# Attention on Trainium2: two PSUM banks for the scores and three for the raw products, with the prior added to the scores first

## The reference

```
x = L0_attn_x                                             # 32 x 256 x 128, float32
x = x + 0.5 * ffn(layernorm(x), ...)                      # routed experts, top 2 of 12 (4 of them zero experts)
x = x + attn(layernorm(x), Wq, bq, Wk, bk, Wv, bv, Wo, bo, prior_lambda)
x = x + 0.5 * ffn(layernorm(x), ...)

# attn, 16 heads of 8, L = 256
Q, K, V = split_heads(x @ Wq.T + bq), ...
scores = einsum('bhqd,bhkd->bhqk', Q, K) / sqrt(8)
scores = scores + prior_lambda * gaussian_mask(256)       # the same for all heads and batches
out = einsum('bhqk,bhkd->bhqd', softmax(scores), V)
return out @ Wo.T + bo
```

## Time and profile before

| | |
|---|---|
| median of 3 runs | 1354.19 us (1350.55 to 1358.74) |
| span of the profiled execution | 1338.4 us |
| PE, DVE, ACT, POOL busy | 75%, 68%, 54%, 46% of the span |
| exponentials (L849) | 512, 595 ns each |
| maxima (L1329) | 512, 685 ns each |
| turns, first score to last exponential | 160.9 to about 1209 us, with six expert blocks in between |

### The profile page before, as it was taken

The page is one execution under the profiler, slowest core; times in us unless marked ns, Lnnn a source line. Parts: engine busy times, 40 slices in busy tenths (PEclk is TensorE's granted clock), DMA queues, the critical chain, the costliest instruction groups (busy, mean ns, idle before and its releaser), DMA issues.

```text
span 1338.4 us, 37494 instructions
## 1 busy us (share of the span) xinstructions
PE 1003.1 (75%) x13558; PEld 656.9 (49%) x13558; DVE 906.0 (68%) x2405; ACT 716.5 (54%) x1486; POOL 621.8 (46%) x697
## 2 busy tenths in 40 slices
PE   1468587788778888888888888898888876774770
PEld 1346243475447544574444754454754465433560
DVE  4548776685566787866887758877867853654524
ACT  1157344567355755667556575555675555442650
POOL 2556256404544544354542544544445445543554
PEclk9989699998788999998999889988999987785886
DMA  8354535352135311362112731123621274130464
GB/s 247 78 125 107 152 98 173 70 131 55 58 68 131 84 52 60 82 149 60 48 58 65 141 87 53 47 61 73 137 81 53 62 162 113 48 90 19 110 145 113
DMA packets 248881, 125.30 MB, mean 94 GB/s; under 512 B 124384, under 2 KB 238925, under 8 KB 248448
## 3 DMA queue, kind: packets, MB, share of 16 engines
q1 hardware_dynamic: 232320, 94.01, 27.2%
q0 software_dynamic: 16384, 28.89, 8.9%
HBM read 36.25 MB, written 65.31 MB: 76 GB/s over the span
## 4 chain that ended last, share of the span: by engine, by line
PE 39%; DVE 27%; issue 15%; ACT 8%; another core or an unknown queue 7%; POOL 2%; DMA 1%; SPq 1%; DVEq 0%; POOLq 0%; ACTq 0%
PE banks L594 10%; DVE row_max L1329 9%; PE banks L623 4%; PE banks L569 3%; ACT probs L849 3%; DVE h_lo L1223 3%; PE banks L561 2%; PE banks L474 2%; ACT h_hi L778 2%; PE banks L431 2%; PE banks L472 2%; PE banks L487 2%; PE banks L490 2%; DVE stats L1094 2%
## 5 line engine op out<-in xcount | busy, mean ns | idle before, releaser
L849 ACT ACTIVATE probs<-banks 128x512 f32<-128x512 f32 x512 | 280.1, 595 | 313.0 <-PE banks L594 270.4
L1329 DVE TENSOR_REDUCE row_max<-banks 128x2 f32<-128x512 f32 x512 | 330.9, 685 | 100.5 <-PE banks L594 65.2
L938 POOL DMA_INDIRECT big<-yg,slots x256 | 255.2, 997 | 278.3 <-ACT y_rows L784 84.0
L924 POOL DMA_INDIRECT xg<-xs,slots x256 | 253.6, 991 | 274.7 <-PE banks L594 167.8
L1223 DVE TENSOR_TENSOR h_lo<-h_f,h_hi 128x512 bf16<-128x512 f32 x198 | 134.5, 688 | 156.7 <-ACT h_hi L778 118.5
L623 PE MATMUL banks<-probs,v_op 128*32 128x256 f32 x2048 | 202.2, 413 | 10.7 <-ACT ot_sb L842 3.0
L569 PE MATMUL banks<-q_op,k_op 32*128 32x256 bf16 x1024 | 152.2, 293 | 64.7 <-issue 46.0
L594 PE MATMUL banks<-band_parts,thirds 96*32 96x296 bf16 (+2 forms) x4096 | 189.7, 294 | 1.3 <-issue 1.3
L487 PE MATMUL banks<-w_all,h_hi 128*128 x792 | 157.6, 229 | 43.1 <-DVE h_lo L1223 21.6
L561 PE MATMUL banks<-k_op,q_in 32*128 32x256 bf16 x1024 | 154.7, 295 | 37.8 <-DVE row_max L1329 31.5
L776 ACT ACTIVATE h_f<-banks 128x512 f32<-128x512 f32 x198 | 119.8, 605 | 114.3 <-PE banks L474 71.5
(11 more groups left out here) (173 smaller groups left out, 1668.6 us busy)
## 6 DMA issues: line engine op xcount, KB each, us to landing
yg<-y_rows SPq DMA_DIRECT2D x198, 128.0 KB
k_op<-kq_kept SPq DMA_DIRECT2D x96, 64.0 KB
q_in<-kq_kept SPq DMA_DIRECT2D x96, 64.0 KB
xg<-zeros SPq DMA_DIRECT2D x2, 2944.0 KB
xg<-xs,slots POOLq DMA_INDIRECT x256
big<-yg,slots POOLq DMA_INDIRECT x256
kq_kept<-kq_hi SPq DMA_DIRECT2D x32, 128.0 KB
kq_kept<-kq_lo SPq DMA_DIRECT2D x32, 128.0 KB
```

The lines of the kernel that those rows point to most:

```text
L849: act.activation(probs[:, q % 2, u % 4, :], banks[:, ST[(16 * b + u) % 3], :], ACT.Exp).then_inc(A["exp_done"], 1)
L924: pool.indirect_dma_start(xg[q], bass.IndirectOffsetOnAxis(slots[:, q % 4, c, t:t + 1], 0), xs[:, q % 2, t, :], None, bounds_check=groups[ ...
L938: pool.indirect_dma_start(y_back[:, i, c, :], None, yg[q], bass.IndirectOffsetOnAxis(slots[:, q % 4, c, t:t + 1], 0)).then_inc(gathered[i] ...
L1329: dve.tensor_reduce(row_max[:, gp, :, qt, j], banks[:, MX[v % 2], :].rearrange("p (k c) -> p k c", k=2), AX.X, ALU.max).then_inc(A["max_do ...
```

## The change

The ring of banks for scores goes from three to two, (0, 1), and the ring for raws from two to three, (2, 3, 4). The waits that guard the banks move with them: a score now waits for the exponential of the unit two before it (three before it till now), and a raw waits for the maximum of the unit three before it (two before it till now). In each step the 16 bands change places: the eight of the scores come first, the eight of the raws second. Nothing is added or taken away.

```diff
-        ST, MX, PV, M = (0, 1, 4), (2, 3), 5, (6, 7)
+        ST, MX, PV, M = (0, 1), (2, 3, 4), 5, (6, 7)
...
-                return pe.matmul(banks[:, MX[v % 2], bass.ts(k, L)],
+                return pe.matmul(banks[:, MX[(16 * rb + v) % 3], bass.ts(k, L)],
...
-                return pe.matmul(banks[:, ST[(16 * b + u) % 3], bass.ts(k, L)], k_op[r:r + 32, par, g, bass.ts(kt, P)],
+                return pe.matmul(banks[:, ST[u % 2], bass.ts(k, L)], k_op[r:r + 32, par, g, bass.ts(kt, P)],
...
-                                wait(pe, A["exp_done"], 16 * b + u + i - 2)
+                                wait(pe, A["exp_done"], 16 * b + u + i - 1)
                             score_half(b, par, u + i, k)
                         if rb is not None:
                             if k == 0:
-                                wait(pe, A["max_done"], 16 * rb + v + i - 1)
-                            raw_half(rpar, v + i, k)
+                                wait(pe, A["max_done"], 16 * rb + v + i - 2)
+                            raw_half(rb, rpar, v + i, k)
...
-                    if raws:
-                        prior_to_raws(v)
                     if main:
                         prior_to_scores(b, 2 * s)
+                    if raws:
+                        prior_to_raws(rb, v)
...
-                            act.activation(probs[:, q % 2, u % 4, :], banks[:, ST[(16 * b + u) % 3], :],
+                            act.activation(probs[:, q % 2, u % 4, :], banks[:, ST[u % 2], :],
```

More of the change, by code:

```diff
@@ L555, in project, with raw_half @@
                 mm.then_inc(A["kq_done"], 1)
-            def raw_half(par, v, k):
+            def raw_half(rb, par, v, k):
                 gp, qt, j = v // 8, v % 8 // 4, v % 4
                 r, g = 32 * j, 2 * gp + k
-                return pe.matmul(banks[:, MX[v % 2], bass.ts(k, L)],
+                return pe.matmul(banks[:, MX[(16 * rb + v) % 3], bass.ts(k, L)],
                                  q_in[r:r + 32, par, g, bass.ts(qt, P)], k_op[r:r + 32, par, g, :],
@@ L601, in prior_to_scores, with prior_to_raws @@
                     for r in range(4):
-                        mm = add_band(ST[(16 * b + u) % 3], u % 8 // 4, r)
+                        mm = add_band(ST[u % 2], u % 8 // 4, r)
                     mm.then_inc(A["st_done"], 1)
-            def prior_to_raws(v0):
+            def prior_to_raws(rb, v0):
                 for v in (v0, v0 + 1):
                     for r in range(4):
-                        mm = add_band(MX[v % 2], v % 8 // 4, r)
+                        mm = add_band(MX[(16 * rb + v) % 3], v % 8 // 4, r)
                     mm.then_inc(A["raw_done"], 1)
@@ L1315, in _ @@
             attention_constants()
-            MX, M = (2, 3), (6, 7)
             def batch_stats(b):
@@ L1328, in maxima @@
                     wait(dve, A["cols_ready"], 2 * b + gp - 1)
-                dve.tensor_reduce(row_max[:, gp, :, qt, j], banks[:, MX[v % 2], :].rearrange("p (k c) -> p k c", k=2),
+                dve.tensor_reduce(row_max[:, gp, :, qt, j], banks[:, MX[(16 * b + v) % 3], :].rearrange("p (k c) -> p k c", k=2),
                                   AX.X, ALU.max).then_inc(A["max_done"], 1)
```

## The result

The changed kernel takes 1346.47 us in the median (1341.83 to 1358.86, 12 runs) against 1354.61 us for the kernel before on the same chip (12 runs): 8.1 us less. The forecast was 1343 us.

The account below looks back on a forecast made before the run. The prediction took a loop of PE waiting for raws' banks and DVE for their bands to bound steps 0 to 2 of light turns; 8.8 us (light) plus 2 us (heavy) off 1354.19 gave 1343.4 us, range 1338 to 1348.

Parts of the forecast that it names:

- The opened loop: Steps 0 to 2 of light turns: PE's raws wait for DVE's maxima, a 2.03 us period that a third raw bank opens.
- the closed one: Steps 0 to 2: with two score banks, the second score waits for the step before's second exponential, a 1.83 us period.
- The 0.23 us for the maxima's later start: Each step: with the raws' bands second, DVE starts its maxima about 0.23 us later than by the old order.
- A free light turn: Light turn without holds: three periods shrink 0.60 us, 0.1 taken off for step 4; gain 0.5 us, bounds 0 and 0.99.
- the chain starts from the bands: After step 3: the path to kq_lo starts from bands, not maxima, so kq_lo comes 0.6 us earlier if a_xt_lo is ready.
- The held turns: Light turns where POOL's DMA delays PE's increments: period 2.09 us, gain 0 to 0.8; 0.4 us mean over 22 light turns, 8.8.
- rival 1: Light turns: held increments and later maxima eat the gain; 0.1 us x 22, nothing in heavy turns, about 1352 us; chance 0.28.
- the heavy ones: Ten turns with two POOL DMAs per step: 0.2 us x 10 = 2 us gain, bounds 0 and 16 us.
- the sum of 8.8 and 2: Whole kernel: 8.8 us from 22 light turns plus 2 us from 10 heavy turns, 10.8 us less.
- What the waits were to show: New profile: PE's raw-bank waits (31.5, 57.4 us) near nothing, PE's score waiting for ACT instead, ACT's 270.4 us band wait falling.
- rival 2: Steps 0 to 3: DVE starves as maxima come later; 15 us price at most, 10 expected, 1364 us; chance 0.16.
- Rival 3: Heavy turns gain as well, ACT and DVE being decoupled by half a step: 14 us there, 1331 us; chance 0.13.

Follow-up runs that it names:

- both halves of the change: The new banks with the old order of bands, and the old banks with the new order, each against the kernel before: ratios 1.0052 and 1.0184.
- without the DMAs: Kernel before and changed kernel, each skipping the 288 indirect DMAs POOL issues during the turns: 1267.3 and 1256.03 us, against 1357.94 us for before with them.
- banks alone: Kernel before with two score banks and three raw banks, the raws' bands still first: 1216.58 us against 1210.75 us for before, ratio 1.0052.
- order alone: Kernel before with its three score banks and two raw banks, but the scores' bands first: 1232.98 us against 1210.75 us for before, ratio 1.0184.
- interleaved: Changed kernel with bands unit by unit (score, raw, score, raw): 1199.13 us against 1210.75 us for before, ratio 0.9908; again on another chip 1347.88 us, 0.9926.
- the first set: Follow-up runs on one chip: the change again 1202.18 us, new banks only 1216.58, new order only 1232.98, unit-by-unit bands 1199.13, before 1210.75.

## Why the prediction was right, and where it was off

**The loops.** The step that carried the forecast was right in kind and size. The opened loop (2.03 us) and the closed one (1.83 us by the sum, 1.81 to 1.82 measured) are confirmed by both halves of the change, whose periods the same terms give (2.06 and 2.26). The 0.23 us for the maxima's later start was 0.22 to 0.25 us. One reading was too smooth: turn 10 was not free, since between 514.69 and 517.11 in the earlier trace rows lie 2.42 us and not 2.03; without the DMAs all three periods are 2.02 to 2.03.

**A free light turn.** Forecast 0.5 us, measured 0.57 (18.50 to 17.93 us), and by the path that was forecast. The bands of steps 0 and 3 of turn 11 (L594 is L602 in these two kernels), without the DMAs, before and then the change, cut the stretch between two kq_lo (above) in three:

```profile
488.64 0.56 PE L602 MATMUL banks<-band_parts,thirds 96*32 96x180 bf16 x13
...
494.71 0.64 PE L602 MATMUL banks<-band_parts,thirds 96*32 96x180 bf16 x16
```

```profile
477.51 0.56 PE L602 MATMUL banks<-band_parts,thirds 96*32 96x180 bf16 x13
...
482.96 0.64 PE L602 MATMUL banks<-band_parts,thirds 96*32 96x296 bf16 x16
```

| us | kq_lo to bands of step 0 | three periods | bands of step 3 to kq_lo |
|---|---|---|---|
| before | 9.46 | 6.07 | 2.97 |
| change | 9.51 | 5.45 | 2.97 |
| banks alone | 9.28 | 6.18 | 2.97 |
| order alone | 9.65 | 6.80 | 2.97 |
| interleaved | 9.28 | 5.45 | 2.97 |

The three periods give 0.62 us (forecast 0.60) and the part behind kq_lo takes 0.05 back (forecast 0.1). The last part is the same in all five kernels, and so are the 1.24 us in it from the bands to the projections: as forecast, the chain starts from the bands, and a_xt_lo does not lead in these turns. In turn 11 of the change it ends at 549.78, and the projections start at 550.15, 0.37 us later, where 0.82 - 0.43 = 0.39 had been reckoned. DVE's wait ahead of kq_lo fell by 0.43 us because the maxima of step 3 moved towards kq_lo; it is not a measure of the gain. Between step 3 and the next step 0 the bands shift, which I had no terms for (3 to 4 takes 0.43 us more, 4 to 5 takes 0.61 less, 5 to 7 takes 0.39 less, 7 to 0 takes 0.61 more), but this nearly cancels. The table also shows what interleaving adds: its 0.23 us are all ahead of step 0.

**The held turns.** This step was right in its numbers and wrong in what it gave. I had forecast a period of 2.09 us with maxima that come with the release; turn 14 shows 2.05 and 2.09 us and maxima at 0.98 us. But the turn gains nothing: from the first bands to kq_lo it took 9.49 us before and takes 9.48 now. Its three periods are 0.5 us shorter in all, and the last part is 0.5 us longer (3.53 us instead of 3.03). The DMA of step 3, released sooner, now covers the end of the projections (670.95, when they end at 671.79), so kq_hi starts 0.57 us after that end; before, the DMA came at their end and kq_hi followed 0.10 us behind. The later a_xt_lo has hardly a part in it: the projections start 1.28 us after the bands, 1.24 before. Such a turn ends as rival 1 says, but by another path. Not all do: on the same stretch turns 13 and 15 gain 0.34 and 0.12 us. What is left over the whole shows in the sums of the light turns that have no expert block between them (17 of the 18; from one start of kq_lo to the next, the last one, from turn 27 to 28, left out):

| 17 light turns, 7 heavy ones, us | before | change | interleaved |
|---|---|---|---|
| chips of 1354 to 1358 us | 351.3, 355.1; 168.4, 169.6 | 349.1; 172.5 | 347.2; 168.3 |
| the same without the paced DMAs | 335.9; 132.1 | 329.1; 127.1 | |
| chip of 1211 us | | 332.0; 129.9 | 327.4; 128.3 |

(Two executions of before in the first row. Banks alone: 339.6; 133.2. Order alone: 346.2; 140.9. The first two of the seven heavy stretches end with the second kq_lo, ahead of turn 0, and with that of turn 0.) With the DMAs these 17 light turns gain 2 to 6 us, where 17 x 0.4 = 6.8 was forecast, and the heavy ones take 3 to 4 us more in the profiled executions, where a gain of 2 was forecast; without the DMAs 6.8 and 5.0 us are gained. So the DMAs, not the nature of the heavy turns, keep those from gaining. The holds alone may not be the whole of it: on the chip of 1211 us, where hardly any increments come late, the change gains 8.6 us and so hardly more than on the first. The medians say 8.1 us in all, which is more than the rows place: expert blocks differ by over 10 us between two executions of before on two chips (five of them with their turns, 381.9 and 393.4 us), and one profile each can't divide 8 us among stretches. That the sum of 8.8 and 2 came within 3 us of the measured gain is therefore in part luck: the term of a free turn is confirmed, the 0.4 us as a mean over held turns and the 2 us of the heavy ones are not.

**The clock.** I had left it out. A turn with a stretch at half the clock loses 0.7 to 1.3 us. In the changed kernel without the DMAs (columns as in the earlier trace rows):

```profile
595.50:615.00 19.50, 16.29 (x303) 9.41 (x296) 17.65 (x43) 11.23 (x23) 2.09 (x4) 0.98 0.12 36
615.00:635.40 20.40, 17.31 (x304) 10.05 (x300) 17.51 (x43) 11.32 (x23) 2.09 (x4) 0.92 0.12 35
613.00:617.60 4.60, 3.46 (x56) 2.02 (x57) 3.28 (x8) 1.19 (x3) 0.00 (x0) 0.65 0.31 87
```

Turns 14 and 15 have the same work, and take 19.50 and 20.40 us; the second begins with a clock of 0.65 in the mean of 4.6 us, so partly at 1.2 and partly at 2.4 GHz. Before without the DMAs the corresponding turn held its clock:

```profile
607.20:627.20 20.00, 17.37 (x303) 9.59 (x298) 17.38 (x43) 11.05 (x22) 2.09 (x4) 1.00 0.12 35
625.00:629.40 4.40, 3.10 (x70) 1.73 (x64) 3.63 (x9) 1.54 (x4) 0.00 (x0) 1.00 0.28 78
```

By the starts of kq_lo, six of the 12 light turns with expert outputs take 20.4 us or more in the changed kernel instead of 19.4, while of before three take over 20.7 instead of 20.0. The clock's rows tell these apart without exception: those six and three have a mean granted clock of 0.92 from one kq_lo to the next, and all the other light turns 1.00. The stretches at 1.2 GHz cost the change about 6 us in these turns and before about 3. That explains a part of the difference between 0.57 us for each of 28 turns, 16 us, and the 11.3 us measured; no run holds the clock fixed. On the chip of the first set such stretches stand in 8 of the 17 light turns with the change and with the banks alone, in 6 interleaved, and in 1 with the order alone, by one profile each.

**What the waits were to show.** PE's wait for the raws' banks fell by two thirds, not to near nothing; ACT's fell as forecast. That PE's score would wait for ACT in its place was not borne out: the wait put down to ACT went from 11.7 to 11.2 us on the matmul and from 19.8 to 9.1 on the weight load. What rose is idle time ahead of the scores that is put down to nobody, from 46.0 to 62.1 and from 107.4 to 145.2 us. DVE's wait for bands, rival 2's sign, rose from 65.2 to 78.4 us, and the kernel got faster all the same.

**The rivals.** Rival 2 is right that later bands for the raws have a price: the order alone costs 1.8%, more than its 15 us. But the price is paid in the maxima's own loop (2.25 us), not through a_xt_lo and the projections, which stand 1.24 us behind the bands there too. The rule of the Trainium skill ("Perfetto Trace Analysis", Optimization Strategy), to make what the most contended engine waits for start sooner, is thus borne out for two banks of raws. With three the price is covered, and what is left of it shows in the interleaved kernel (17.70 against 17.93 us). By the same section a repeating bubble can be a lack of PSUM. Here banks alone did not cure it, as the bank taken from the scores closed their loop. Rival 3 did not occur with the DMAs in place. Of the versions tried the interleaved one has the lowest ratios (0.9908 and 0.9926), though on neither kind of chip can it be told from the change by them.

## What to carry to other kernels

Where two rings of banks are fed by one engine, write down the round trip of each (work on the bank, release, next product, last touch, hand-over) and give the spare bank to the longer one, then put the work on the ring left with fewer banks first in the producer's queue, or alternate the two unit by unit, which cost nothing here. The two moves are to be made and judged together: here each alone was a loss and both were a gain. And before a gain of half a per cent is read from a profile, compare two executions of the unchanged kernel, turn by turn.

## What the runs showed of the hardware that I had not expected

The same program took 1210.75 us on the chip of the first set, and 1354.61 to 1357.94 us in the first measurement and the other two sets. There, PE's semaphore increments come late while POOL issues an indirect DMA. Worked out over all records of a run, the increments of PE's matmuls that ended 0.6 to 1.2 us into such a DMA were more than 0.2 us late in 57 to 77% of cases, against 1 to 5% on the chip of 1210.75 us, with DMAs of the same length. Of the increments of matmuls that ended over 2 us behind the start of the last such DMA, 1 to 4% were late on either kind of chip. Leaving 288 of them out (-90.6 us) shows that the DMAs cause the loss there; it doesn't separate the late increments from anything else that the DMAs do, and why one chip is free of the delay stays open.
